# The four mask transposes of a chunk, one behind each row tile of the even pair

## What is computed

```python
h = jnp.maximum(_layernorm(x, axis=-1), 0.0)
h1 = h @ a[:d]
h2 = h @ a[d:]
e = jax.nn.leaky_relu(h1 + h2.T, negative_slope=0.01)
attention = jnp.where(adj > 0, e, NEG_BIG)
attention = jax.nn.softmax(attention, axis=1)
return x + attention @ h
```

## Time and profile before

| | |
|---|---|
| median of three runs | 1687.62 us |
| the profiled execution | 1690.27 us |
| its span | 1688.5 us |
| PE busy | 1630.9 us, 97% |
| DVE busy | 1440.1 us, 85% |
| ACT busy | 1164.5 us, 69% |
| POOL busy | 220.4 us, 13% |
| the 1024 mask transposes (line 567) on PE | 154.7 us, 272 ns the median one |
| PE waiting for `w_lo` | 28.9 us in 14 waits, all in block 0 |
| PE waiting for a mask | 4.1 us in 3 waits, all in block 0 |
| PE waiting for the first `r` | 17.8 us, once |
| chain that ended last, by engine | PE 89%, DVE 8% |

### The profile page before, as it was taken

The page is one execution under the profiler, slowest core; times in us unless marked ns, Lnnn a source line. Parts: engine busy times, 40 slices in busy tenths (PEclk is TensorE's granted clock), DMA queues, the critical chain, the costliest instruction groups (busy, mean ns, idle before and its releaser), DMA issues.

```text
span 1688.5 us, 40886 instructions
## 1 busy us (share of the span) xinstructions
PE 1630.9 (97%) x13504; PEld 1621.2 (96%) x13504; DVE 1440.1 (85%) x2008; ACT 1164.5 (69%) x1158; POOL 220.4 (13%) x309
## 2 busy tenths in 40 slices
PE   4887999999999999999999999999999999999998
PEld 3777999999999999999999999999999999999998
DVE  6999888888888888888888888888888888888887
ACT  5777766767676666767677676766767676676764
POOL 4667301001010100101010010101001010100100
PEclk9999999999999999999999999999999999999999
DMA  6443455555555555555555555555555455555552
GB/s 199 146 147 112 164 173 182 191 166 185 171 198 174 165 191 167 197 174 187 175 172 186 174 199 168 180 174 185 187 173 184 167 196 174 172 192 167 192 173 88
DMA packets 142672, 294.08 MB, mean 174 GB/s; under 512 B 4928, under 2 KB 5440, under 8 KB 142656
## 3 DMA queue, kind: packets, MB, share of 16 engines
q1 hardware_dynamic: 138336, 278.15, 49.4%
q10 hardware_dynamic: 4320, 15.73, 2.5%
HBM read 285.47 MB, written 8.39 MB: 174 GB/s over the span
## 4 chain that ended last, share of the span: by engine, by line
PE 89%; DVE 8%; issue 2%; DMA 1%; DVEq 0%; ACT 0%; POOL 0%; SPq 0%; ACTq 0%
PE acc L609 28%; PE acc L612 27%; PE acc L611 27%; PE T L567 6%; DVE rep L460 3%; DVE w_lo L481 2%; DVE W L471 1%; DVE bst L442 1%; PE rep L582 0%; DMA r_rep<-in_L_gnn_a_dram 0%; DVE mv L447 0%; DMA xb<-in_x_dram 0%; ACT hb L307 0%; DVE adj_in L552 0%; DVE adj_in L547 0%
## 5 line engine op out<-in xcount | busy, mean ns | idle before, releaser
L609 PE MATMUL acc<-h_hi,w_hi 128*128 (+1 forms) x4096 | 1186.2, 290 | 28.9 <-DVE w_lo L481 28.9
L612 PE MATMUL acc<-h_hi,w_lo 128*128 (+1 forms) x4096 | 1159.2, 283 | 0.0
L611 PE MATMUL acc<-h_lo,w_hi 128*128 (+1 forms) x4096 | 1153.8, 282 | 0.0
L350 ACT ACTIVATE w_hi<-W 128x1024 fp32r<-128x1024 f32 x512 | 540.5, 1059 | 420.3 <-DVE W L471 367.0
L609 PEld LDWEIGHTS acc<-h_hi,w_hi 128*128 128x128 f32 x4096 | 776.3, 190 | 33.5 <-issue 33.1
L471 DVE SCALAR_TENSOR_TENSOR W<-r_rep,g_all,T 128x512 f32<-128x512 int8 (+1 forms) x1024 | 720.1, 745 | 103.3 <-DVE w_lo L481 90.5
L611 PEld LDWEIGHTS acc<-h_lo,w_hi 128*128 128x128 f32 x4096 | 781.1, 191 | 0.2
L612 PEld LDWEIGHTS acc<-h_hi,w_lo 128*128 128x128 f32 x4096 | 777.4, 190 | 0.0
L481 DVE SCALAR_TENSOR_TENSOR w_lo<-W,w_hi 128x1024 fp32r<-128x1024 f32 x512 | 627.7, 1226 | 123.4 <-PE acc L612 109.4
L341 ACT ACTIVATE mask<-adj_in,mhalf 128x2048 fp8e5<-128x2048 int32 x256 | 509.2, 1989 | 24.7 <-issue 23.2
L271 POOL TENSOR_TENSOR xb<-xb,stage 128x256 f32<-128x256 f32 x60 | 41.3, 689 | 1381.6 <-ACT hb L379 1361.3
(11 more groups left out here) (58 smaller groups left out, 277.5 us busy)
## 6 DMA issues: line engine op xcount, KB each, us to landing
adj_in<-in_adj_dram SPq DMA_DIRECT2D x256, 1024.0 KB, 5.2
xb<-in_x_dram ACTq DMA_DIRECT2D x15, 512.0 KB, 3.2
out_dram<-xb ACTq DMA_DIRECT2D x15, 512.0 KB, 2.6
xb<-in_x_dram SPq DMA_DIRECT2D x8, 512.0 KB, 3.3
xo<-in_x_dram SPq DMA_DIRECT2D x8, 512.0 KB, 3.3
adj_in<-in_x_dram SPq DMA_DIRECT2D x1, 512.0 KB, 3.2
out_dram<-adj_in SPq DMA_DIRECT2D x4, 128.0 KB, 1.9
r_rep<-in_L_gnn_a_dram SPq DMA_DIRECT2D x1, 256.0 KB, 6.0
```

What stands on the lines that cost most here:

```text
L350: nc.scalar.activation(w_hi[:, k % HL, :], W[:, k % 2, :], ACT.Relu).then_inc(s_hi, 1)
L609: nc.tensor.matmul(acc[:, t, 0:WC], w_hi[:, k % HL, cols], rhs_hi, start=start and u == 0, stop=False)
L611: nc.tensor.matmul(acc[:, t, 0:D], w_hi[:, k % HL, cols], rhs_lo, start=False, stop=False)
L612: last = nc.tensor.matmul(acc[:, t, 0:WC], w_lo[:, k % LL, cols], rhs_hi, start=False, stop=stop and u == 1)
```

## The change

`transpose_mask` takes a list of row tiles. It waits only when tile 0 is in the list, and raises `s_T` only when tile 3 is. `products` calls it behind each row tile of an even pair, with that one tile. The other calls, before the first pair of all, stay as they were. Behind tile 3, `s_used` is raised by the last product, ahead of the last transpose.

```diff
-            def transpose_mask(n, kc, wait):
+            def transpose_mask(n, kc, wait, tiles=range(G)):
 
                 g = n * CI + kc
-                pe.wait_ge(s_mask, g + 1)
-                if wait:
-                    pe.wait_ge(s_w, 2 * (g - 1))
-                for t in range(G):
+                if 0 in tiles:
+                    pe.wait_ge(s_mask, g + 1)
+                    if wait:
+                        pe.wait_ge(s_w, 2 * (g - 1))
+                for t in tiles:
                     last = nc.tensor.transpose(T[:, kc, t * P:(t + 1) * P], mask_words[:, kc, t, :], ident[:])
-                last.then_inc(s_T, 1)
+                if G - 1 in tiles:
+                    last.then_inc(s_T, 1)
...
-            def products(b, c, g, k, start, stop, fresh):
+            def products(b, c, g, k, start, stop, fresh, n_next):
...
                     if stop and t < G - 1:
                         last.then_inc(s_acc, 1)
-                last.then_inc(s_used, 1)
+                    if t == G - 1:
+                        last.then_inc(s_used, 1)
+                    if n_next is not None:
+                        transpose_mask(n_next, k // 2, True, [t])
...
-                    products(b, c, n * PI + k, k, first and k == 0, last and k == PI - 1, first_block)
-                    if k % 2 == 0 and not (last_block and last):
-                        transpose_mask(n + 1, kc, True)
+                    spread = k % 2 == 0 and not (last_block and last)
+                    products(b, c, n * PI + k, k, first and k == 0, last and k == PI - 1, first_block,
+                             n + 1 if spread else None)
```

## The result

| | before | changed |
|---|---|---|
| median of four runs | 1688.02 us | 1738.53 us |
| lowest and highest | 1687.58, 1690.16 | 1738.16, 1739.68 |
| profiled execution, span | 1690.27, 1688.5 | 1738.16, 1736.4 |

The changed kernel is slower: ratio 1.0295, 95% interval 1.0282 to 1.0308. The medians lie 50.5 us apart, the two profiled spans 47.9; the profiled execution of before happens to be one of its longest. What follows accounts for the 47.9.

The account below looks back on a forecast made before the run. From block 1 on PE alone was taken to set the end. Boundary waits of 30.4 + 2.3 + 2.8 + 1.7 = 37.2 us on the median 1687.62 gave 1725 us, range 1716 to 1742.

Parts of the forecast that it names:

- Four lone transposes cost as much as four in a row, 0: Even pairs on PE: each transpose costs 0.11 us alone or grouped, four make 0.44 as before, difference 0.
- the 7 us that the rounding of the rows left open: Some 240 chunks behind block 0: three more switches each, rows read to 0.01 us, bound of 7 us either way.
- The first chunk of a block, 2.03: Blocks 1 to 15: mask late by 1.77 us, with PE start-up 2.03 each, 30.4 us in all.
- The last chunk but one, 0.20: Blocks 1 to 14: mask in time by 0.06 us but not by the 0.26 start-up; 0.20 each, 2.8 in all.
- the last, 0.12: Last chunk, blocks 1 to 14: `L273` starts before `w_lo` and ends 0.95 us sooner; 0.12 each, 1.7 in all.
- rival 1: Last chunk of a block: `L273` held up as before, costing 15.0 us; total 1738, up to 1745; chance 0.2.
- The second chunk of a block, 0: Mask conversion assumed not to slip with PE's later arrival: 0; if it slipped, 0.51 us each, 7.7 in all.
- Block 0, 0: Block 0: mask waits are given back, since the odd pair behind waits for `w_lo` anyway; cost 0.
- the wait in pair 28 (forecast 2.3): Block 0's last iteration: mask late by 2.02 us plus 0.26 start-up, 2.3 us.
- The clock stays at 1.00: PE's granted clock at the boundary waits: expected to stay at 1.00, adding nothing to the sum.
- Rival 2: PE's clock falls behind the new 2.03 us waits: 15 x 1.4 = 21 us more, 1746 us; chance 0.06.
- The other side (lone transposes hide): Even pairs: next weights load during a long product, lone transposes cost half, 53 us come back, 1672 us; chance 0.06.

Follow-up runs that it names:

- experiment 3: The change, but transposes kept together in each block's first and last iteration from block 1 on and in block 0's last iteration: 1693.87 us, ratio 1.0031.
- experiment 1: The kernel before, with only the two waits moved forward behind row tile 0 and the four transposes still together behind the pair: 1739.55 us, ratio 1.0296.
- experiment 7: The change, with PE made to wait for the mask before the first product of blocks 1 to 14: 1757.45 us, ratio 1.0405.
- experiment 4: The change, but with transposes 0 and 1 behind row tile 1 and 2 and 3 behind row tile 3: 1713.17 us, ratio 1.0144.
- experiment 5: The change, with ACT converting the mask between the evacuations of row tiles 0 and 1 at a block's start: 1702.57 us, ratio 1.0080.
- experiment 6: The change, but with the transposes kept together in the last chunk but one of blocks 1 to 15: 1745.39 us, ratio 1.0334.
- Experiment 2: The change, but transposes kept together in the first chunk of blocks 1 to 15 and the last iteration of every block: 1699.88 us, ratio 1.0065.
- experiment 8: The change, with 14 unread products ahead of the mask wait in the first chunk of blocks 1 to 14: 1731.07 us, ratio 1.0251.

## Why the prediction was right, and where it was off

Right: the direction, the place and the mechanism. The range of 1716 to 1742 holds 1738.5. The forecast of 1725 was 13.5 us low. By its steps:

- *Four lone transposes cost as much as four in a row, 0.* Wrong by 0.026 to 0.028 us a chunk, about 6 us in all (experiment 3). It is within the 7 us that the rounding of the rows left open, but I took the middle of a bound where a switch could hardly be cheaper.
- *The first chunk of a block, 2.03.* Right: the late mask is 1.76, the start-up of the transpose 0.14 and not 0.26, and 0.11 more are lost in the two products behind it, 2.00 in all. I had read the start-up from `L609`, a product. A product behind the mask starts 0.23 and 0.35 behind it in experiments 1 and 7; which of the instructions between the wait and the product make the difference is not shown. Experiments 1, 4 and 5 show this wait without the spread, shorten it and take it away, each at its price.
- *The last chunk but one, 0.20, and the last, 0.12.* 0.14 and 0.09 measured, the lone transposes included. The masks are there 0.08 us before they are wanted, in both. The chain behind the second number (three transposes inside the even pair, `w_lo` behind `L273`, `L273` at its own pace) is shown by the earlier trace rows against the trace after, and by experiment 6, which turns it back. Without this step the forecast would have been 13 us higher, and nearer the measured time for a wrong reason: rival 1 named 1738, but its `L273` was not held up.
- *The second chunk of a block, 0.* Right for the change: its conversion at 511.46 was done at 513.45 and wanted at 514.19. Experiment 2 shows the wait that was covered.
- *Block 0, 0.* The traces differ by 1.8 up to its end, with 2.1 for the wait in pair 28 (forecast 2.3). Pair 27 was quick and pair 28 slow, which cancel.
- *The clock stays at 1.00.* This is the step that failed. Rival 2 held in part: it fell in five of the 15 pairs and not in all or none, 7.5 us. I had put the new waits "in between" the two kinds of the earlier trace rows and then taken the better end, with 0.06 for the other, so that none of the 21 us went into the sum.
- *The other side (lone transposes hide).* No: each costs 0.113, and the load of the next weights still starts with the transpose and not before it (603.55 both, in the timeline above).

With the measured sizes: 30.0 for the first chunk + 2.1 for block 0's wait + 3.2 for the last two chunks + 4.7 for the steady ones + 7.5 for the clock = 47.5, against 47.9 in the spans. The forecast had 37.2. The 10.7 that it lacks are the clock's 7.5 and the transposes' 6, less some 3 by which it had the waits and block 0 too high. That it stayed in the range owes something to a width chosen for other errors, rival 1 above all. The medians' 50.5 has 2.6 us more because the profiled execution of the kernel before was a long one; no step accounts for that.

## What to carry to other kernels

Spreading a group of instructions in an in-order queue moves the group's *wait* forward with its first member. Before doing it, look up when each releaser comes, at the boundaries above all and not in the steady chunk: here 18 products stood behind a wait that was free in 13 of 16 chunks and late at the block's start by 1.8 us, because another engine's queue had evacuations ahead of the conversion. And follow a late releaser back over all engines: here `w_lo` went from 0.14 us ahead of `L273` to 0.34 behind it, which changed which of POOL and DVE was held up, and with it 0.95 us on ACT.

## What the runs showed of the hardware

- The granted clock fell from 1.00 to 0.50 (2.4 to 1.2 GHz) in some PE waits of 1.8 to 2.0 us, in 5, 8 and 1 of 15 in three kernels, in 9 of 14 of 2.8 us, in none of 30 of 0.9 to 1.4. A fall cost 1.5 us here. Useless products in the wait prevented it and made the kernel 7.5 us faster (experiment 8). What picks the waits that lose the clock stays open; with the change it was every second block, so that the moment at which a wait comes may count beside its length.
- A GpSimd addition with 256 elements a partition took 0.74 us, or 1.69 to 1.70 when a `w_lo` with two SBUF inputs had started 0.12 to 0.14 before it; when it started first by 0.34 it kept its 0.74 and `w_lo` took 1.48 instead of 1.23. A copy of four elements took 0.18 or 1.19 in the same way.
- From the end of ACT's conversion to the start of a transpose that waits for it were 0.14 us in the rolled loops, and 0.05 where the code is written out (block 15: 1.81 in place of 1.90). To the start of a product were 0.23 us (experiment 1) and 0.35 us (experiment 7).
- A transpose between two products took 0.113 us of PE's time, one in a row of four 0.110, and the load of the product's weights behind it began with it.
